# Split keys stacked from GpSimd's queue, split queries from SyncE's: four layers of attention on one core

## The chip, the cores and the metric

The program runs on one core of a Trainium2 chip. The metric is the device time of one execution in microseconds (us). One core has TensorE (PE) for matrix products, VectorE (DVE), ScalarE (ACT), GpSimd (POOL) and SyncE (SP). SP does no arithmetic here: its queue only issues transfers (DMAs). The DMA engines are shared by whoever issues.

## The reference

Sixteen batches of a 256 x 128 input pass through four layers. Layers 0, 2 and 3 hold attention with 16 heads of 8 channels; layer 1 is a mixture of experts with single-head attention. Cut to what matters here (heads are written out as an axis `h`):

```
q = (norm(x) @ Wq + bq)            # 256 queries, heads of 8
k = (norm(src) @ Wk + bk)          # 256 keys (self) or 1601 keys (cross, from the context)
v = (norm(src) @ Wv + bv)
attn = softmax(q @ k.T * 8**-0.5)  # per head, exact maximum subtracted
x = x + gate * (attn @ v @ Wo + bo)
```

Layer 0 is self attention, then cross attention with an MLP; layer 2 is cross attention; layer 3 is self attention, then cross attention with an MLP.

## The kernel before, in words

The program has four parts in a row: a small one that works out modulation columns, an attention phase `pa` (layer 0), the expert layer `moe` (layer 1) and an attention phase `pb` (layers 2 and 3). Only the two attention phases contain the change. Each runs two streams at once: `c`, the cross attention (1601 keys), and `z`, the self attention (256 keys). In `pa` both streams have 16 items (an item is one batch of one layer). In `pb` stream `c` has 32 (layer 2's batches, then layer 3's) and `z` has 16.

The work of a phase is cut into tokens: `S` and `T` are scores with their exponential, `V` the product with the values, `M` and `Rn` the maxima of the scores, `ln` a layer norm, `xt` a transpose of its result by PE, `q`, `k`, `v` the projections, `ca` the norm of the context, `ctx` its transposes, `proj` the output projection, `ln2`, `x2t`, `h`, `fc2` the MLP. `body_plan` writes down at which fraction of a steady body each token stands and of which item. A body is one round, in which the scores of one item of each stream are made while the next items are prepared. `stage_list` and `merge_maxima` turn that into one list, `PROG`. Every engine walks the same `PROG` in order, does the part of each token that is its own, and waits on semaphores for the others.

A query or key in f32 is split into three bf16 parts. ACT writes the projection to `kf`; POOL splits it into `ksp` (lines 914 to 920, token `k`), and likewise `qf` into `qsp` (lines 902 to 906, token `q`). The parts are then stacked on partitions by DMAs, so that one bf16 product gives the sum of six partial products: token `kq` (lines 597 to 610) issues 12 DMAs into `qst` and 12 into `kst`. Each moves 64 rows. A key row has 1601 numbers in stream `c` and 256 in `z`; a query row has 256. The stacks are double buffered, so `kq` of item i waits until PE has read the last score of item i - 2 (`last_score`).

Per body the order in `PROG` around the change is this. At the boundary of two bodies stand the last scores, `T` of `c`, and at once `kq` of `c` and `kq` of `z`. Then follow, among scores, values and maxima that concern only PE, ACT and DVE:

- in `pb`: `ln` of `c`, `ln` of `z`, `xt` of `c` (PE waits for `xn`, which POOL writes at line 887), `proj` of `c`, `q` of `c`, `xt` of `z`, `ca`, `proj` of `z`
- in `pa`: `ln` of `z`, `proj` of `c`, `ln2` of `c` (DVE waits for `x1`, which POOL writes at line 934), `xt` of `z`, `ca`, `proj` of `z`, `x2t` of `c`
- some 100 tokens after `kq`: the first `M` of the new item, where PE waits for both stacks (lines 1027 and 1028).

Each phase begins with bodies in which not all of this is present. `pa` has three bodies with a `z` item alone, then 13 with both streams at `kq`, then 3 with `c` alone. `pb` has 16 `kq` points with both streams and 16 with `c` alone.

Of the kernel before, what the change touches and what calls it, by code (L numbers as in the profile page):

```python
# [31 lines left out]
ROWS = 64  # L32
MAX_ROW = 62
K_PART = (0, 0, 0, 1, 1, 2)
# [14 lines left out]
def wait(eng, sem, value):  # L49

    if isinstance(value, int) and value < 1:
        return
    eng.wait_ge(sem, value)
# [121 lines left out]
K_ROWS = 48  # L175
# [250 lines left out]
def attention_phase(nc, nm, streams, cols_d, rows_d, ident_d, late_x, fill_late):  # L426
# [31 lines left out]
    def a_done(tok, s, i):  # L458

        return na[tok, s.key, i] + 1  # L460

    def last_score(s, i):
        return a_done(("T", QUADS - 1) if s.last < P else ("S", QUADS - 1, s.kt // 2 - 1, 1), s, i)

    with Semaphores(nc) as sems, ExitStack() as ctx:
# [3 lines left out]
        def sem(name):  # L469
            return sems(f"{nm}_{name}")  # L470
# [10 lines left out]
        for j, spec in enumerate(specs):  # L481
            w = spec.w = Weights()
# [60 lines left out]
        a_full, a_free = sem("act_ring_full"), sem("act_ring_free")  # L543
# [7 lines left out]
        @block.sync  # L551
        def _(sp):
            def const(dst, src, slow=False):
                sp.dma_start(dst, src, allow_slow_non_contiguous=slow).then_inc(consts, 16)

            def col(v):
                return v.rearrange("(c p) -> p c", p=P)

            def rows(v):
                return v.rearrange("(o n) -> o n", o=1).to_broadcast([P, D])  # L560

            const(ident[:], ident_d)
            for spec in specs:
                w = spec.w
                for dst, src in ((w.wq, spec.wq), (w.wk, spec.wk), (w.wv[:], spec.wv), (w.wo[:], spec.wo)):
                    const(dst, src)
                const(w.brow[:, 0, :], spec.bq.rearrange("(o n) -> o n", o=1))
                const(w.brow[:, 1, :], spec.bk.rearrange("(o n) -> o n", o=1))
                const(w.bv[:], col(spec.bv), slow=True)
                const(w.bo_rows[:], rows(spec.bo))  # L570
                if spec.mlp:
                    const(w.w1[:], spec.mlp["w1"])
                    const(w.w2[:], spec.mlp["w2"].rearrange("(c p) n -> p c n", p=P))
                    const(w.b1[:], col(spec.mlp["b1"]), slow=True)
                    const(w.b2_rows[:], rows(spec.mlp["b2"]))

            for tok, s, i in PROG:
                k, (spec, n), w = tok[0], s.items[i], i % 2
                if k == "ldx":
                    if spec.after:  # L580
                        key, first = spec.after
                        sp.wait_ge(by_key[key].x_out, 16 * (first + n + 1))
                    wait(sp, s.x_ln, i * QT)
                    sp.dma_start(s.xin[:], spec.x_src[n].rearrange("(t p) d -> p t d", p=P)).then_inc(s.x_in, 16)
                elif k == "lda":
                    if i:
                        sp.wait_ge(a_free, a_done(("xt",), s, i - 1))
                        if s.has_ctx:
                            sp.wait_ge(a_free, a_done(("ctx", len(s.groups) - 1), s, i - 1))
                    sp.dma_start(s.acols[:], cols_d[n]).then_inc(s.a_cols, 16)  # L590
                elif k == "ldc":
                    if i:
                        sp.wait_ge(a_full, a_done(("ctx", len(s.groups) - 1), s, i - 1))
                    src, kt = spec.ctx[n], s.kt
                    sp.dma_start(s.cin[:, 0:kt - 1, :], src[0:(kt - 1) * P, :].rearrange("(t p) d -> p t d", p=P)).then_inc(s.c_in, 16)
                    sp.dma_start(s.cin[0:s.last, kt - 1, :], src[(kt - 1) * P:s.keys, :]).then_inc(s.c_in, 16)
                elif k == "kq":
                    sp.wait_ge(s.filled, s.fills)
                    if i >= 2:
                        sp.wait_ge(a_full, last_score(s, i - 2))  # L600
                    sp.wait_ge(s.q_sp, i + 1)
                    for t in range(6):
                        for par in range(2):
                            lo = par * ROWS
                            sp.dma_start(s.qst[w][lo + t:lo + K_ROWS:6, :, :], s.qsp[lo:lo + ROWS, Q_PART[t], :]).then_inc(s.q_st, 16)
                    sp.wait_ge(s.k_sp, i + 1)
                    for t in range(6):
                        for par in range(2):
                            lo = par * ROWS
                            sp.dma_start(s.kst[w][lo + t:lo + K_ROWS:6, :, :], s.ksp[lo:lo + ROWS, K_PART[t], :]).then_inc(s.k_st, 16)  # L610
                elif k == "mr":
                    half = tok[1]
                    sp.wait_ge(a_free, a_done(("Rt", half), s, i))
                    for par in range(2):
                        at = par * ROWS + MAX_ROW
                        sp.dma_start(s.qst[w][at:at + 2, 4 * half:4 * half + 4, :], s.mrow[half][par * 8:par * 8 + 8, :]).then_inc(s.m_st[half], 16)
                elif k == "ldr":
                    wait(sp, s.d_x1, i)
                    wait(sp, s.d_x2, s.mlp_to[i])
                    sp.dma_start(s.xres[:], spec.x_src[n].rearrange("(t p) d -> p t d", p=P)).then_inc(s.x_res, 16)  # L620
                    if spec.gate is not None:
                        sp.dma_start(s.gate[:], rows_d[n][spec.gate:spec.gate + 1, :].to_broadcast([P, D])).then_inc(s.x_res, 16)
                    if spec.mlp:
                        sp.dma_start(s.dcols[:], cols_d[n]).then_inc(s.x_res, 16)
                        sp.dma_start(s.dgate[:], rows_d[n][spec.mlp["gate"]:spec.mlp["gate"] + 1, :].to_broadcast([P, D])).then_inc(s.x_res, 16)
                elif k == "st":
                    dst = spec.x_dst[n].rearrange("(t p) d -> p t d", p=P)
                    if spec.mlp:
                        sp.wait_ge(s.d_x2, s.mlp_to[i] + 1)
                        sp.dma_start(dst, s.x2[:]).then_inc(s.x_out, 16)  # L630
                    else:
                        sp.wait_ge(s.d_x1, i + 1)
                        sp.dma_start(dst, s.x1[:]).then_inc(s.x_out, 16)
            for s in streams:
                sp.wait_ge(s.x_out, 16 * len(s.items))

        @block.vector
        def _(dve):
# [41 lines left out]
            for tok, s, i in PROG:  # L680
                k, (spec, n) = tok[0], s.items[i]
                if k == "M":
                    _, p, u = tok
                    segs = s.units[u]
                    cnt, width = len(segs), segs[0][2]
# [177 lines left out]
        def _(pool):  # L863
# [10 lines left out]
            for tok, s, i in PROG:  # L874
                k, (spec, n) = tok[0], s.items[i]
                w = spec.w
# [30 lines left out]
                elif k == "k":  # L907
# [12 lines left out]
                    ins = pool.tensor_tensor(s.ksp[:, 2, part], s.kf[:, part], s.ksp[:, 1, part], ALU.subtract)  # L920
                    if tok[1] == len(s.groups) - 1:
                        ins.then_inc(s.k_sp, 1)
                elif k == "proj":
                    pool.wait_ge(a_free, a_done(tok, s, i))
                    pool.wait_ge(s.x_res, s.res_to[i + 1] * 16)
# [45 lines left out]
        def _(pe):  # L971
# [9 lines left out]
            for tok, s, i in PROG:  # L981
                k, (spec, n), b2 = tok[0], s.items[i], i % 2
                w = spec.w
                if k in ACT_RING:
                    N = na[tok, s.key, i]
                    dst = aunit[N % RING_A]
                    wait(pe, a_free, N - RING_A + 1)
                if k == "S":
                    _, q, j, pp = tok
                    pair = 2 * q + pp  # L990
                    if j == 0 and pp == 0 and q % 2 == 0:
# [8 lines left out]
                elif k == "T":  # L1000
# [6 lines left out]
                    ins.then_inc(a_full, 1)  # L1007
                elif k == "V":
                    _, q, t = tok
                    tail = s.last < P and t == s.kt - 1  # L1010
                    if t == 0:
# [813 lines left out]
```

## Time and profile before

| | |
|---|---|
| median of 3 runs | 5429.4 us (5426.66 to 5432.44) |
| the profiled execution | 5426.89 us, span of the trace 5425.1 us |
| PE busy | 4676.3 us (86% of the span) |
| DVE busy | 4123.3 us (76%) |
| ACT busy | 3587.5 us (66%) |
| POOL busy | 1673.2 us (31%) |
| mean granted TensorE clock | 0.965 of full speed |

The profile counts an engine's compute instructions as busy, not its waits and not the issuing of DMAs. The span is the time from the first to the last instruction; the execution's own time is 1.8 us longer.

### The profile page before, as it was taken

The page shows a single profiled execution, that of the slowest core. Times are in us where ns is not written, and L with a number is a line of the kernel's source. Part 1 is how long each engine was busy: PE and PEld are TensorE (multiplying, and loading weights), DVE is VectorE, ACT ScalarE, POOL GpSimd, SP SyncE. Part 2 cuts the span into 40 slices and gives each one's busy share as a digit, 9 for nine tenths or more (in the row PEclk, how much of TensorE's full clock was granted, in tenths as well). Part 3 has the DMA queues.
Part 4 walks back from the last instruction along what each step waited for, and adds up shares of the span by engine and source line. Part 5 has one row for each costly group of instructions (what it writes and reads, how often), then busy time and mean ns, then how long its engine had stood idle before and what let it go on. Part 6 is the DMA issues. An engine that isn't in the chain of part 4 may idle for free.

```text
span 5425.1 us, 123295 instructions
## 1 busy us (share of the span) xinstructions
PE 4676.3 (86%) x47956; PEld 2196.8 (40%) x47956; DVE 4123.3 (76%) x8997; ACT 3587.5 (66%) x4899; POOL 1673.2 (31%) x2339
## 2 busy tenths in 40 slices
PE   4689889889998588867989999999999998989987
PEld 2234433433433377752333333333333343333333
DVE  4588888888878244445888888888888887887884
ACT  1377777777777344423777777777777777777776
POOL 3444343343341100024232423233222223232321
PEclk9799999999999899986999999999999999999998
DMA  2211211211210111102112111121211111211110
GB/s 52 68 52 54 68 44 54 67 44 52 61 39 25 45 33 33 33 25 64 52 51 66 55 58 55 53 66 54 67 56 53 51 48 50 62 43 53 42 46 7
DMA packets 362976, 271.12 MB, mean 50 GB/s; under 512 B 47911, under 2 KB 325002, under 8 KB 362396
## 3 DMA queue, kind: packets, MB, share of 16 engines
q1 hardware_dynamic: 362396, 263.23, 17.0%
q8 instruction: 383, 6.28, 0.5%
q14 instruction: 197, 1.61, 0.1%
HBM read 86.96 MB, written 12.78 MB: 18 GB/s over the span
## 4 chain that ended last, share of the span: by engine, by line
PE 36%; ACT 7%; DVE 6%; issue 5%; POOL 1%; SPq 0%; DMA 0%; ACTq 0%; POOLq 0%; DVEq 0%
PE pb_obank L1021 13%; PE pb_dbank L1034 8%; ACT pb_probs L772 6%; DVE pb_c_maxs L693 5%; PE pb_aunit L997 5%; PE pb_aunit L1068 2%; PE pb_aunit L1075 2%; PE pb_dbank L1082 1%; PE pb_aunit L1060 1%; PE pb_aunit L1108 1%; PE pb_aunit L1102 1%; PE pb_aunit L1005 1%; ACT pb_c_kf L815 1%; PE pb_aunit L1051 0%; PE pb_aunit L1092 0%
## 5 line engine op out<-in xcount | busy, mean ns | idle before, releaser
L693 DVE TENSOR_REDUCE pb_c_maxs<-pb_dbank 128x1 f32<-128x512 f32 (+1 forms) x3584 | 2044.5, 627 | 411.6 <-PE pb_dbank L1034 397.1
L772 ACT ACTIVATE pb_probs<-pb_aunit 128x1024 f32<-128x1024 f32 (+1 forms) x1792 | 1744.5, 1024 | 380.4 <-PE pb_aunit L997 344.8
L693 DVE TENSOR_REDUCE pa_c_maxs<-pa_dbank 128x1 f32<-128x512 f32 (+1 forms) x1792 | 1025.8, 627 | 180.2 <-PE pa_dbank L1034 170.5
L772 ACT ACTIVATE pa_probs<-pa_aunit 128x1024 f32<-128x1024 f32 (+1 forms) x960 | 934.8, 1026 | 198.1 <-PE pa_aunit L997 174.8
L1021 PE MATMUL pb_obank<-pb_probs,pb_c_vaug 128*9 128x256 f32 x13312 | 953.2, 384 | 6.3 <-ACT pb_probs L772 5.5
L1034 PE MATMUL pb_dbank<-pb_c_kst,pb_c_qst 62*128 62x512 bf16 (+1 forms) x4096 | 780.5, 344 | 77.1 <-DVE pb_c_maxs L693 67.7
L997 PE MATMUL pb_aunit<-pb_c_qst,pb_c_kst 64*128 64x256 bf16 x6144 | 570.1, 273 | 61.1 <-ACT pb_probs L772 43.1
L1034 PEld LDWEIGHTS pb_dbank<-pb_c_kst,pb_c_qst 62*128 62x128 bf16 x4096 | 233.6, 93 | 632.8 <-DVE pb_c_maxs L693 433.2
L1021 PE MATMUL pa_obank<-pa_probs,pa_c_vaug 128*9 128x256 f32 x6656 | 481.2, 385 | 6.2 <-ACT pa_probs L772 5.8
L1034 PE MATMUL pa_dbank<-pa_c_kst,pa_c_qst 62*128 62x512 bf16 (+1 forms) x2048 | 396.8, 345 | 53.8 <-DVE pa_c_maxs L693 42.6
L1021 PEld LDWEIGHTS pb_obank<-pb_probs,pb_c_vaug 128*9 128x9 f32 x13312 | 245.1, 89 | 375.3 <-issue 214.4
L997 PEld LDWEIGHTS pb_aunit<-pb_c_qst,pb_c_kst 64*128 64x128 bf16 x6144 | 253.2, 95 | 309.8 <-ACT pb_probs L772 134.1
L879 POOL TENSOR_SCALAR pb_c_rs_v<-pb_c_agg 128x2 f32<-128x2 f32 x32 | 7.9, 246 | 1032.9 <-DVE pb_c_agg L714 1032.9
L997 PE MATMUL pa_aunit<-pa_c_qst,pa_c_kst 64*128 64x256 bf16 x3072 | 285.5, 272 | 36.4 <-ACT pa_probs L772 25.9
L1034 PEld LDWEIGHTS pa_dbank<-pa_c_kst,pa_c_qst 62*128 62x128 bf16 x2048 | 115.4, 93 | 331.1 <-DVE pa_c_maxs L693 213.2
L693 DVE TENSOR_REDUCE pa_z_maxs<-pa_dbank 128x2 f32<-128x512 f32 x256 | 163.9, 686 | 107.7 <-PE pa_dbank L1034 107.7
L1021 PEld LDWEIGHTS pa_obank<-pa_probs,pa_c_vaug 128*9 128x9 f32 x6656 | 121.4, 89 | 191.0 <-issue 111.4
L997 PEld LDWEIGHTS pa_aunit<-pa_c_qst,pa_c_kst 64*128 64x128 bf16 x3072 | 122.6, 95 | 168.8 <-ACT pa_probs L772 91.6
L693 DVE TENSOR_REDUCE pb_z_maxs<-pb_dbank 128x2 f32<-128x512 f32 x256 | 164.6, 685 | 23.6 <-PE pb_dbank L1034 23.4
L914 POOL CAST pb_c_ksp<-pb_c_kf 128x1024 bf16<-128x1024 f32 x64 | 54.6, 852 | 288.6 <-ACT pb_c_kf L815 288.6
L1526 DVE SCALAR_TENSOR_TENSOR moe_hh<-moe_ht,moe_hz 128x512 f32<-128x512 f32 x48 | 33.2, 692 | 123.6 <-ACT moe_ht L1620 123.6
L926 POOL TENSOR_TENSOR pb_c_x1a<-pb_c_x1a,pb_l_cross_bo_rows 128x256 f32<-128x256 f32 x32 | 23.2, 724 | 337.0 <-ACT pb_c_x1a L842 337.0
(475 smaller groups left out, 6680.3 us busy)
## 6 DMA issues: line engine op xcount, KB each, us to landing
pb_c_kst<-pb_c_ksp SPq DMA_DIRECT2D x384, 200.1 KB
pa_c_kst<-pa_c_ksp SPq DMA_DIRECT2D x192, 200.1 KB
pb_c_cin<-in_ctx SPq DMA_DIRECT2D x32, 768.0 KB
pa_c_cin<-in_ctx SPq DMA_DIRECT2D x16, 768.0 KB
moe_cin<-in_ctx SPq DMA_DIRECT2D x16, 768.0 KB
pb_c_qst<-pb_c_qsp SPq DMA_DIRECT2D x384, 32.0 KB
pa_z_qst<-pa_z_qsp SPq DMA_DIRECT2D x192, 32.0 KB
pa_z_kst<-pa_z_ksp SPq DMA_DIRECT2D x192, 32.0 KB
```

The costliest lines, as they stand in the source:

```text
L693: dve.tensor_reduce(dst, dbank[N % RING_D][:, 0:cnt * width].rearrange("p (s c) -> p s c", s=cnt), AX.X, ALU.max).then_inc(d_free, 1)
L772: act.activation(probs[u % RING_P][0:rows].rearrange("p a i q -> p (a i q)"), src[0:rows, :], ACT.Exp, scale=HD ** -0.5).then_inc(a_free, 1)
L815: act.activation(s.kf[:, at:at + width], src[:, 0:width], ACT.Identity, bias=w.bk[:]).then_inc(a_free, 1)
L914: pool.tensor_copy(s.ksp[:, 0, part], s.kf[:, part]).then_inc(s.k_hi, 1)
L997: ins = pe.matmul(dst[:, par * 512 + h * NQ:par * 512 + (h + 1) * NQ], s.kst[b2][lo:lo + ROWS, pair, t * P:(t + 1) * P], s.qst[b2][lo:lo + ...
L1005: ins = pe.matmul(dst[0:s.last, par * 512 + pp * NQ:par * 512 + (pp + 1) * NQ], s.kst[b2][lo:lo + ROWS, 2 * q + pp, (s.kt - 1) * P:s.keys] ...
L1021: ins = pe.matmul(obank[32 * h4:32 * h4 + HD + 1, half * NQ:(half + 1) * NQ], s.vaug[i % 2][:, t, 4 * q + h4, :], src, start=(t == 0), sto ...
L1034: ins = pe.matmul(dbank[nd[tok, s.key, i, par] % RING_D][:, col:col + width], s.qst[b2][lo:lo + MAX_ROW, p, qt * P:(qt + 1) * P], s.kst[b2 ...
L1060: ins = pe.transpose(dst[:, (t - t0) * P:(t - t0) * P + rows], s.cin[0:rows, t, :], ident[0:rows, 0:rows])
L1068: ins = pe.matmul(dst[:, at - t0 * P:at - t0 * P + width], w.wkp[:], src[:, at:at + width], start=True, stop=True)
L1075: ins = pe.matmul(dst[0:rows, (t - t0) * P:(t - t0 + 1) * P], (s.srct if s.has_ctx else s.xmt)[:, t * P:t * P + rows], w.wv[:], start=True ...
L1082: ins = pe.transpose(dbank[N % RING_D][:, g * P:(g + 1) * P], s.osb[:, g, qt * P:(qt + 1) * P], ident[:])
```

## The change

`kq` now appears on two engines. SP keeps the 12 DMAs of the queries, with their waits. POOL's branch of `PROG` gets a `kq` of its own: it waits for the fills of the stacks, for the last score of item i - 2 and for its own last split of the keys, and then issues the same 12 key DMAs from POOL's queue. Nothing that computes is changed.

```diff
                         for par in range(2):
                             lo = par * ROWS
                             sp.dma_start(s.qst[w][lo + t:lo + K_ROWS:6, :, :], s.qsp[lo:lo + ROWS, Q_PART[t], :]).then_inc(s.q_st, 16)
-                    sp.wait_ge(s.k_sp, i + 1)
-                    for t in range(6):
-                        for par in range(2):
-                            lo = par * ROWS
-                            sp.dma_start(s.kst[w][lo + t:lo + K_ROWS:6, :, :], s.ksp[lo:lo + ROWS, K_PART[t], :]).then_inc(s.k_st, 16)
                 elif k == "mr":
...
                         ins.then_inc(s.k_sp, 1)
+                elif k == "kq":
+                    w = i % 2
+                    pool.wait_ge(s.filled, s.fills)
+                    if i >= 2:
+                        pool.wait_ge(a_full, last_score(s, i - 2))
+                    pool.wait_ge(s.k_sp, i + 1)
+                    for t in range(6):
+                        for par in range(2):
+                            lo = par * ROWS
+                            pool.dma_start(s.kst[w][lo + t:lo + K_ROWS:6, :, :], s.ksp[lo:lo + ROWS, K_PART[t], :]).then_inc(s.k_st, 16)
                 elif k == "proj":
```

## Rows read from the trace of the kernel before

**Rows 1.** Windows, one body of pb with both streams
```profile
core 0: us, PE busy (x) PEld busy (x) DVE busy (x) ACT busy (x) POOL busy (x), PEclk, DMA share, GB/s
3518.70:3613.70 95.00, 86.48 (x977) 36.45 (x969) 82.59 (x187) 71.80 (x91) 31.92 (x49) 1.00 0.20 58
```

**Rows 2.** Instructions of line 610: issue times in ns, and who waited
```profile
L610 SPq DMA_DIRECT2D pb_c_kst<-pb_c_ksp x384: 611/1018/1871, 2467.3 to 5258.8; - x192
L610 SPq DMA_DIRECT2D pb_z_kst<-pb_z_ksp x192: 612/612/761, 2798.5 to 4223.6; - x192
...
  ACT pa_z_kf L815: 20.6, 3
  PE pa_dbank L1034: 9.4, 1
  PE pb_dbank L1034: 3.6, 1
```

**Rows 3.** Waits of SP's queue: us in total, times, longest
```profile
SPq L616 <- ACT pb_c_mrow L833: 1311.0, 64, 39.9
```

**Rows 4.** Timeline of SP around kq, the same body of pb
```profile
3517.30 1.26 SPq L616 DMA_DIRECT2D pb_c_qst<-pb_c_mrow  x2
3518.68 7.96 SPq L605 DMA_DIRECT2D pb_c_qst<-pb_c_qsp  x12
3526.69 12.88 SPq L610 DMA_DIRECT2D pb_c_kst<-pb_c_ksp  x12
3539.68 8.38 SPq L605 DMA_DIRECT2D pb_z_qst<-pb_z_qsp  x12
3548.10 8.15 SPq L610 DMA_DIRECT2D pb_z_kst<-pb_z_ksp  x12
3569.05 1.36 SPq L616 DMA_DIRECT2D pb_c_qst<-pb_c_mrow  x2
```

**Rows 5.** Timeline of POOL, the same body
```profile
3530.67 0.25 POOL L879 TENSOR_SCALAR pb_c_rs_v<-pb_c_agg 128x2 f32<-128x2 f32 x1 [38.92 <-DVE pb_c_agg L714]
...
3532.16 0.88 POOL L887 TENSOR_SCALAR pb_c_xn<-pb_c_xin,pb_c_rs_m,pb_c_rs_y 128x128 f32<-128x128 f32 x2
...
3554.94 2.46 POOL L894 TENSOR_TENSOR pb_c_cs_y<-pb_c_cs_v,pb_mhalf 128x13 f32<-128x13 f32 x1
```

**Rows 6.** Timeline of PE, same body: last score, xt of c, first M of new item
```profile
3518.20 0.41 PE L1005 MATMUL pb_aunit<-pb_c_qst,pb_c_kst 64*65 64x256 bf16 x4
...
3539.10 0.44 PE L1047 MATMUL pb_aunit<-pb_ident,pb_c_xn 128*128 128x128 f32 x2 [0.30 <-ACT pb_c_vaug L827]
...
3566.60 0.39 PE L1034 MATMUL pb_dbank<-pb_c_kst,pb_c_qst 62*128 62x512 bf16 x2
```

**Rows 7.** Timelines of SP, POOL, DVE and PE, one body of pa
```profile
841.59 7.90 SPq L605 DMA_DIRECT2D pa_c_qst<-pa_c_qsp  x12
...
944.09 7.90 SPq L605 DMA_DIRECT2D pa_c_qst<-pa_c_qsp  x12
...
956.19 0.24 POOL L879 TENSOR_SCALAR pa_z_rs_v<-pa_z_agg 128x2 f32<-128x2 f32 x1 [25.23 <-DVE pa_z_agg L714]
...
957.67 0.88 POOL L887 TENSOR_SCALAR pa_z_xn<-pa_z_xin,pa_z_rs_m,pa_z_rs_y 128x128 f32<-128x128 f32 x2
967.01 0.73 POOL L926 TENSOR_TENSOR pa_c_x1a<-pa_c_x1a,pa_l_cross_bo_rows 128x256 f32<-128x256 f32 x1 [8.46 <-ACT pa_c_x1a L842]
967.81 0.74 POOL L934 TENSOR_TENSOR pa_c_x<-pa_c_x1a,pa_c_xres 128x256 f32<-128x256 f32 x1
...
973.00 0.47 DVE L744 BATCH_NORM_STATS2 pa_c_st<-pa_c_x 128x6 f32<-128x128 f32 x2
...
973.17 0.44 PE L1047 MATMUL pa_aunit<-pa_ident,pa_z_xn 128*128 128x128 f32 x2 [0.68 <-ACT pa_probs L772]
```

**Rows 8.** Timelines of SP and PE, one body of pb with c alone
```profile
4722.99 7.93 SPq L605 DMA_DIRECT2D pb_c_qst<-pb_c_qsp  x12
...
4740.87 0.44 PE L1047 MATMUL pb_aunit<-pb_ident,pb_c_xn 128*128 128x128 f32 x2 [0.46 <-ACT pb_c_vaug L827]
...
4808.44 7.90 SPq L605 DMA_DIRECT2D pb_c_qst<-pb_c_qsp  x12
```

**Rows 9.** Timeline of all engines, start of pb
```profile
2467.27 12.72 SPq L610 DMA_DIRECT2D pb_c_kst<-pb_c_ksp  x12
2467.33 0.25 POOL L879 TENSOR_SCALAR pb_c_rs_v<-pb_c_agg 128x2 f32<-128x2 f32 x1
...
2469.87 0.66 PE L1047 MATMUL pb_aunit<-pb_ident,pb_c_xn 128*128 128x128 f32 x2 [9.89 <-POOL pb_c_xn L887]
...
2486.22 0.61 PE L1034 MATMUL pb_dbank<-pb_c_kst,pb_c_qst 62*128 62x512 bf16 x2 [3.57 <-DMA pb_c_kst<-pb_c_ksp]
```

**Rows 10.** Timeline of all engines, start of pa
```profile
62.88 0.67 POOL L920 TENSOR_TENSOR pa_z_ksp<-pa_z_kf,pa_z_ksp 128x256 bf16<-128x256 f32 x1
...
69.43 10.77 POOL L867 MEMSET pa_c_kst<- 128x12808 bf16 x1
...
83.68 0.67 POOL L920 TENSOR_TENSOR pa_z_ksp<-pa_z_kf,pa_z_ksp 128x256 bf16<-128x256 f32 x1
...
90.81 0.69 PE L1047 MATMUL pa_aunit<-pa_ident,pa_z_xn 128*128 128x128 f32 x2 [0.69 <-ACT pa_probs L772]
```

**Rows 11.** Waits of all engines, first 350 us
```profile
ACT pa_z_qf L794 <- DMA pa_z_qst<-pa_z_qsp: 23.9, 3, 17.5
```

## The prediction

> **What bounds the kernel now.** I read the window of one whole body first, then who waits for the stacks, then SP's waits, and last the timelines of SP, POOL and PE around the point where the key transfers are issued.
>
> In a steady body of pb PE is busy 86.5 us of 95.0, DVE 82.6, ACT 71.8 and POOL 31.9, at full granted clock [rows 1]. So PE sets the pace, in the order of its list. The key transfers don't touch it: PE waited for a key stack exactly twice in the whole run, 9.4 and 3.6 us, both at the start of a phase; ACT waited for it three times, 20.6 us together, at the start of pa [rows 2]. SP isn't short of time either: it spent 1311 us waiting at its next job, the rows of maxima [rows 3]. In the body shown its 48 issues end at 3556.3 and its next issue is at 3569.05 [rows 4]. Taking 24 of the 48 away from SP therefore gives nothing in a steady body.
>
> **What the change puts on POOL.** A POOL that is busy 31.9 us of 95 looks free, but what counts is where its idle time lies. It finished its last split at 3491.7 (3530.67 less the 38.92 it was idle) and next works at 3530.67, on c's layer norm [rows 5]. Its new DMAs can't use the first 27 us of that gap. They wait for the last score of the item that used the buffer before, which PE finishes at 3518.20 + 0.41 = 3518.6 [rows 6]; SP began at 3518.68 for the same reason [rows 4]. Both streams have their `kq` there, so 24 issues run back to back on POOL from 3518.6, and the norms of c and z stand behind them in its queue.
>
> **The price of one issue.** No row shows a DMA issued by POOL. The bounds come from the nearest rows:
> - from below, SP's issue of the same 64 rows where nothing holds it back: 0.61 us [rows 2];
> - from above, the longest POOL instruction on few elements: 2.46 us [rows 5].
>
> I take 1.02 us, the median of SP's issue of the c keys [rows 2]. It lies nearer to the lower end because the job is the same, 64 rows on each side. I take it for z too, since a queue that is served by software should pay by the row and not by the byte. So 12 issues are 12.2 us and 24 are 24.5 us.
>
> The Trainium skill bears on this in "DMA: Bandwidth & Descriptors", Specifications and SWDGE vs HWDGE: DMAs from GpSimd get their descriptors from code on GpSimd's own cores, those from SP from dedicated hardware, with first bytes after about 1 us against about 0.6. The 0.61 us of SP's row agrees with the second figure; the first would make 24 issues 24 us, an estimate from that page and close to mine. That GpSimd's cores do the issuing is what puts the norms behind it; no run here shows that yet.
>
> **pb, both streams (16 points).** c's norm takes from 3530.67 to 3532.16 + 0.88 = 3533.04, 2.4 us, and PE takes its result at 3539.10 [rows 5, 6]. Room for issues: 3539.1 - 3518.6 - 2.4 = 18.1 us. Needed 24.5, so PE stands 6.4 us in each such body. I count it in full. PE is the engine that sets the pace, DVE and ACT can't run ahead of it by more than their few banks, and the next batch of issues hangs on PE's own last score, so the delay moves on with it. 16 x 6.4 = 102 us.
>
> **pa, both streams (13 points).** c's norm stands elsewhere in that list. First after the issues come z's norm (2.4 us) and then c's x1 (1.5 us, two instructions). DVE wants x1 at 973.0 and PE z's norm at 973.17, with issues from 944.1 on [rows 7]. The tighter room is 973.0 - 944.1 - 2.4 - 1.5 = 25.0 us, needed 24.5: nothing lost, and only 0.5 us to spare.
>
> **c alone (16 points in pb, 3 in pa).** Room: 4740.9 - 4723.0 - 2.4 = 15.5 us [rows 8]; needed 12.2. Nothing lost.
>
> **Start of pb.** The split ends, 12 issues take 12.2 us, and only then comes the norm that began at 2467.33 and for which PE waited 9.89 us. PE's first maxima stood 3.57 us for the key stack anyway [rows 9]. So 12.2 - 3.6 = 9 us.
>
> **Start of pa.** The first z items pass one after the other through split, issue, norm, transpose and split, with little else to do. POOL has its split ready at 63.6, then 12 issues, a norm and the fills of c's stacks, whose last one ran from 69.43 to 80.2 and will now end some 12 us later. The split that ended at 84.35 ends at 96.6, 12 more issues bring 108.8, the norm 111.2, and PE transposes at about 111 in place of 90.81: 20 us late [rows 10]. Some of that comes back. ACT had waited 20.6 us for z's key stacks [rows 2] and 23.9 for z's query stacks, which stood in SP's queue behind the c keys [rows 11]. Two more batches of issues follow. I take 20 us net, with 0 and 49 (four batches of 12.2, nothing given back) as the ends.
>
> **Sum.** 102 + 0 + 0 + 9 + 20 = 131 us on the profiled execution's 5426.9 us, 5558. The median of the runs is 2.5 us above that execution, so I say 5560 us.
>
> The landing of the keys isn't a term. In a c body they are all issued by 3518.6 + 24.5 = 3543, earlier than SP's last at 3556.3 [rows 4], and even SP's were never waited for in a steady body [rows 2].
>
> **The rivals.**
> - *Not slower.* If one issue on POOL costs 0.75 us or less, or if issuing doesn't occupy the cores that compute, 24 issues fit in the 18.1 us of pb and no body is stretched. What is left is the start of pa, where keys and queries are now issued side by side and ACT's waits of 44.5 us shrink, against POOL's later norms. Time: 5415 to 5435. For it speaks SP's 0.61 us; against it that POOL would have to issue nearly as fast. The skill's rule for this ("DMA: Bandwidth & Descriptors", Issuing engines are not separate DMA queues) is that issuing from several engines saves only sequencer time, usually small. Taken alone it says no change, since the row of SP's waits shows that its time is free.
> - *A dearer issue, and pa is bound too.* From 1.04 us on pa's 13 bodies pay as well, from 1.29 us (15.5 / 12) those with c alone. At 1.4 us: 16 x (33.6 - 18.1) = 248, 13 x (33.6 - 25.0) = 112, 16 x (16.8 - 15.5) = 21, starts 45: 426 us, 5855. At the upper bound of 2.46 us the same lines give 654 + 442 + 224 + 80, some 6830 us. For it speaks that POOL's short instructions cost more than their data explain, 0.25 us for two columns and 2.46 for thirteen [rows 5]; against it that nothing else about 64 rows is slow.
> - *The keys land late.* If a transfer issued by POOL took so long that the last were in after the first maxima of the new item, PE would wait at line 1028. They have from 3543 to the first maxima at 3566.6, over 23 us [rows 6], where SP needs 12.9 us for all twelve of c [rows 4]. I give it little.
>
> **How the numbers follow.** Forecast, an issue between 0.75 and 1.25 us: 0.62, by itself 5445 to 5730 (at 1.25: 190 + 65 + 45 = 300 us). Dearer issue: 0.24. Not slower: 0.11. Late keys or something else: 0.03. The range runs from 5450 to 5860: it leaves out the not-slower case and most of what lies beyond 1.4 us. A difference of 0.2% (11 us) is about what a measurement of this kernel can tell from none. The not-slower case splits into 0.03 faster and 0.06 same, its remainder being a small loss at the starts; so slower has 0.91.
>
> **What would show it.** In the trace of the changed kernel: POOL's queue with DMA issues of about 1 us, 12 or 24 in a row, beginning at PE's last score; c's norm in pb starting some 24 us after it; PE waiting some 6 us at line 1047 for `pb_c_xn` in 16 bodies, each about 101 us long; bodies of pa at 102.5 us as before (841.59 to 944.09) and those with c alone at 85.4 [rows 7, 8]. Wrong would be an issue time far from 1.02 us (each 0.1 us is worth 38 us, above 1.04 us 70), a stall that PE makes up for later in the body, or bodies of pa stretched at an issue time below 1.04 us.

## The result and the profile after

The changed kernel takes 5450.9 us (median of 5 runs, 5449.3 to 5452.5) against 5430.6 us (5426.7 to 5432.9) for the kernel before, run beside it: a ratio of 1.0036 with a 95% interval from 1.0024 to 1.0048. It is slower, as I forecast, but by 20 us and not by 131. 5450.9 lies at the lower edge of my range, and that is chance: as shown below, what slows the kernel stands in none of my terms.

First the price of one issue. In the view of the new line 927 on POOL, the three numbers are shortest, median and longest issue in ns; below them stand idle times of POOL ahead of these instructions, in us and times.

```profile
L927 POOL DMA_DIRECT2D pb_c_kst<-pb_c_ksp x384: 562/562/667, 2472.2 to 5270.3; - x192
L927 POOL DMA_DIRECT2D pa_z_kst<-pa_z_ksp x192: 561/561/769, 63.6 to 1367.1; - x192
...
  issue: 502.9, 36
  PE pb_aunit L1010: 446.3, 17
```

One issue takes 0.56 us, for 200 KB of c and for 32 KB of z alike. That is below SP's fastest, 0.61 [rows 2], which I had taken for the lower bound. Twelve take 6.8 us and twenty-four 13.4.

The windows view of the body that answers to [rows 1], then POOL's and PE's timelines around it [rows 5, 6] and SP's [rows 4]:

```profile
3535.10:3630.10 95.00, 86.48 (x977) 36.53 (x977) 82.62 (x186) 71.79 (x91) 45.30 (x73) 1.00 0.26 58
```
```profile
3535.64 6.77 POOL L927 DMA_DIRECT2D pb_c_kst<-pb_c_ksp  x12 [27.46 <-PE pb_aunit L1010]
3542.40 6.64 POOL L927 DMA_DIRECT2D pb_z_kst<-pb_z_ksp  x12
3549.12 0.25 POOL L874 TENSOR_SCALAR pb_c_rs_v<-pb_c_agg 128x2 f32<-128x2 f32 x1
```
```profile
3534.66 0.41 PE L1010 MATMUL pb_aunit<-pb_c_qst,pb_c_kst 64*65 64x256 bf16 x4
3555.55 0.44 PE L1052 MATMUL pb_aunit<-pb_ident,pb_c_xn 128*128 128x128 f32 x2 [0.30 <-ACT pb_c_vaug L822]
```
```profile
3535.14 14.16 SPq L605 DMA_DIRECT2D pb_c_qst<-pb_c_qsp  x12
3549.41 7.82 SPq L605 DMA_DIRECT2D pb_z_qst<-pb_z_qsp  x12
```

POOL is busy 13.4 us more, which are its 24 issues (on POOL the profile counts them as busy), and PE, DVE and ACT are busy as before, within 0.03 us, in the same 95.0 us. The order of events is the forecast one: 24 issues from the last score on, then c's norm. But the norm starts 14 us after the score, not 24, and PE takes its result 20.9 us after that score began, as in [rows 6]. SP now needs 14.2 us for c's queries in place of 8.0, with key transfers beside them; in pb nobody waits for a query stack.

So where do 25.6 us of span (5450.7 against 5425.1) come from? The two profiled executions lie 5 us further apart than the medians. I took from SP's timeline of both traces when the query issues of each item of c begin, and subtracted:

```
item of c, stage            before     after      later by
7th body of pa              739.00     737.24     -1.8
12th body of pa             1251.36    1249.31    -2.1
first of pb                 2455.06    2459.06     4.0
third of pb                 2608.81    2617.03     8.2
third body with z           2949.02    2958.20     9.2
the next                    3043.96    3060.44    16.5
eight bodies on             3803.88    3820.32    16.4
the next                    3898.05    3920.29    22.2
last                        5238.58    5263.62    25.0
```

The loss is made at a few places: between the stages, in the start of pb, and in two single bodies of pb with both streams. The other bodies of that kind cost nothing. The body that begins at 2958.2 shows what those two have in common. POOL's timeline, then PE's, then windows of PE with its granted clock (the number behind the busy time):

```profile
2958.71 6.77 POOL L927 DMA_DIRECT2D pb_c_kst<-pb_c_ksp  x12 [27.45 <-PE pb_aunit L1010]
2965.47 2.77 POOL L927 DMA_DIRECT2D pb_z_kst<-pb_z_ksp  x5
2976.84 3.88 POOL L927 DMA_DIRECT2D pb_z_kst<-pb_z_ksp  x7 [8.60 <-issue]
2980.79 0.25 POOL L874 TENSOR_SCALAR pb_c_rs_v<-pb_c_agg 128x2 f32<-128x2 f32 x1
```
```profile
2983.31 0.66 PE L1052 MATMUL pb_aunit<-pb_ident,pb_c_xn 128*128 128x128 f32 x2 [5.35 <-POOL pb_c_xn L882]
```
```profile
2980.00:2982.00 2.00, 0.00 (x0) 1.00 0.24 66
2982.00:2984.00 2.00, 0.69 (x6) 0.50 0.00 0
...
2988.00:2990.00 2.00, 2.00 (x22) 0.79 0.00 0
2990.00:2992.00 2.00, 2.00 (x23) 1.00 0.00 0
```

After its 17th issue in this body POOL pauses for 8.6 us, for no reason that the profile names. With the pause the issues last 22.0 us; that is more than the room of 18.1, and PE waits 5.35 us for the norm. Behind that idle stretch its granted clock is 0.50, which is 1.2 GHz, until about 2989; in the kernel before it is 1.00 from 2561 to 4480, through all bodies of this kind. Wait and clock together make the body 102.2 us long instead of 94.9. The other long body, at 3820.3, has its pause (7.86 us) behind the 17th issue too.

Counting POOL's key transfers through the trace, a pause stands behind the 113th of a phase and then behind every 108th: 8 in all. Four, behind five issues of a body, took 2.0 us each, as this one:

```profile
3440.70 2.89 POOL L927 DMA_DIRECT2D pb_c_kst<-pb_c_ksp  x5 [27.44 <-PE pb_aunit L1010]
3445.62 3.88 POOL L927 DMA_DIRECT2D pb_c_kst<-pb_c_ksp  x7 [2.03 <-issue]
```

The other four took 7.9 to 9.3 us. Only two of those fell into a pb body with both streams, where there is no room for them. The one in pa (9.3 us at 859) is covered by the 25.0 us there, and that of 8.1 us at 5101, in a body with c alone, takes 14.8 us with its 12 issues, out of a room of 15.5: PE didn't wait for the norm.

The start of pb answers to [rows 9], on POOL and PE:

```profile
2472.16 6.77 POOL L927 DMA_DIRECT2D pb_c_kst<-pb_c_ksp  x12 [0.62 <-POOL pb_c_ksp L915]
2479.00 0.25 POOL L874 TENSOR_SCALAR pb_c_rs_v<-pb_c_agg 128x2 f32<-128x2 f32 x1
```
```profile
2481.53 0.66 PE L1052 MATMUL pb_aunit<-pb_ident,pb_c_xn 128*128 128x128 f32 x2 [17.25 <-POOL pb_c_xn L882]
```

The norm stands behind 6.8 us of issues; PE waits 17.25 us in place of 9.89, and no longer for the keys. Net of the 3.57 us that it waited for them before, that is 3.8. By SP's query issues, the second item of pb begins 4.3 us later against the kernel before than the first did.

Last, the boundary from pa to the next stage, in the timelines of the kernel before and of the changed one: the last store of pa, and POOL's first instruction behind it.

```profile
1819.55 0.37 SPq L630 DMA_DIRECT2D x_after<-pa_c_x  x1
1822.78 0.10 POOL L1633 MEMSET moe_mhalf<- 128x2 f32 x1 [3.25 <-POOLq L85]
```
```profile
1820.62 0.37 SPq L625 DMA_DIRECT2D x_after<-pa_c_x  x1
1826.83 0.10 POOL L1638 MEMSET moe_mhalf<- 128x2 f32 x1 [6.24 <-POOLq L85]
```

Line 85 is the barrier at the end of a stage, behind the handing back of its semaphores. POOL stands there 3.0 us longer.

### The profile page after: what moved, and what is told of

Read it like the earlier page. It is cut to its first block, busy times and chain, and to the rows that moved or that the text cites. A ratio compares the mean times of both kernels' runs of the same rounds, so it can differ in the third digit from the quotient of the medians.

```text
span 5450.7 us, 123375 instructions
## 1 busy us (share of the span) xinstructions
PE 4689.4 (86%) x47956; PEld 2201.9 (40%) x47956; DVE 4129.8 (76%) x8997; ACT 3588.2 (66%) x4899; POOL 2209.1 (41%) x3299
## 4 chain that ended last, share of the span: by engine, by line
PE 36%; ACT 7%; DVE 6%; issue 5%; POOL 2%; ACTq 0%; DMA 0%; SPq 0%; POOLq 0%; DVEq 0%
PE pb_obank L1026 13%; PE pb_dbank L1039 8%; ACT pb_probs L767 5%; DVE pb_c_maxs L688 5%; PE pb_aunit L1002 5%; PE pb_aunit L1073 2%; PE pb_aunit L1080 2%; PE pb_aunit L1065 1%; PE pb_dbank L1087 1%; PE pb_aunit L1113 1%; PE pb_aunit L1107 1%; PE pb_aunit L1010 1%; ACT pb_c_kf L810 1%; PE pb_aunit L1056 0%; PE pb_aunit L1097 0%
## 5 line engine op out<-in xcount | busy, mean ns | idle before, releaser
L927 POOL DMA_DIRECT2D pb_c_kst<-pb_c_ksp x384 | 216.5, 571 | 730.0 <-PE pb_aunit L1010 446.3
L688 DVE TENSOR_REDUCE pb_z_maxs<-pb_dbank 128x2 f32<-128x512 f32 x256 | 164.6, 685 | 24.5 <-PE pb_dbank L1039 24.3
L927 POOL DMA_DIRECT2D pa_c_kst<-pa_c_ksp x192 | 108.3, 571 | 184.3 <-issue 184.3
```

Source lines behind the costliest of these rows:

```text
L688: dve.tensor_reduce(dst, dbank[N % RING_D][:, 0:cnt * width].rearrange("p (s c) -> p s c", s=cnt), AX.X, ALU.max).then_inc(d_free, 1)
L927: pool.dma_start(s.kst[w][lo + t:lo + K_ROWS:6, :, :], s.ksp[lo:lo + ROWS, K_PART[t], :]).then_inc(s.k_st, 16)
```

## The experiments

The theory from the two traces: issuing takes 0.56 us and fits in the room, so most bodies are free; what is lost is lost where something else stands in POOL's list beside the issues (a norm in the start of pb, a pause in two bodies), and at the boundary. Nine kernels test it and its rivals; the first four were written from these two traces, the others from what came before them.

**z's issues behind the norms.** In pb, POOL's list keeps `kq` of c where it is and gets that of z behind the next norm of z:

```
-            for tok, s, i in PROG:
+            for tok, s, i in pool_order(PROG, nm):     # pb: ("kq") of z put behind the next ("ln") of z
```

> In pb, POOL's list has the issues of z's keys behind the layer norms of c and z; c's keys stay ahead of them. Nothing else is moved. Theory (issuing fits in the room, and what is lost in the two long bodies at 2958 and 3820 us is POOL's pause of some 8 us, which pushes c's norm past the point where PE wants it): only 12 issues (6.8 us) and at most one pause (9 us) stand ahead of the norm, 16 of the 18.1 us of room, so both bodies are back at 95 us and the time is 5436 to 5441 us. Rival (the loss is made by transfers that run beside each other, or by PE's clock, not by POOL's order): the same number of transfers and issues, so 5448 to 5453 us, and long bodies as before.

Measured: 5438.9 us (11 runs, 5434.1 to 5442.2), ratio 1.0011 (1.0003 to 1.0020). POOL and PE in the body that was long:

```profile
2958.25 6.79 POOL L943 DMA_DIRECT2D pb_c_kst<-pb_c_ksp  x12 [27.41 <-PE pb_aunit L1026]
2969.38 0.25 POOL L890 TENSOR_SCALAR pb_c_rs_v<-pb_c_agg 128x2 f32<-128x2 f32 x1 [4.34 <-DVE pb_c_agg L725]
...
2974.14 2.87 POOL L943 DMA_DIRECT2D pb_z_kst<-pb_z_ksp  x5
2978.69 3.89 POOL L943 DMA_DIRECT2D pb_z_kst<-pb_z_ksp  x7 [1.69 <-issue]
```
```profile
2977.80 0.44 PE L1068 MATMUL pb_aunit<-pb_ident,pb_c_xn 128*128 128x128 f32 x2 [0.30 <-ACT pb_c_vaug L838]
```

Both long bodies are back at 94.9 and 94.2 us, and the same transfers are made. So it was POOL's order. The time came as expected. The pause itself is shorter too: 1.7 us behind 5 issues of z, where c's twelve ended 9 us earlier.

**pb alone.** In pa SP issues the keys again.

```
+                    if nm == "pa":
+                        ... the key transfers on sp, as before the change
-                elif k == "kq":
+                elif k == "kq" and not (nm == "pa"):
```

> In pa SP issues the keys as before the change, in pb POOL does. Theory: the change loses 3.0 us at the boundary from pa to the next stage (a gap of 6.2 us in place of 3.3, where POOL's queue is closed) and wins about as much at the start of pa, where keys and queries go out side by side; so the time stays at 5448 to 5453 us, the gap at the boundary is 3.3 us again and pa begins its steady part some 3 us later. Rival (the start of pa costs, as I forecast, and is hidden in the sum by something else): 5431 to 5440 us.

Measured: 5452.0 us (5 runs, 5446.2 to 5454.2), ratio 1.0034 (1.0022 to 1.0047). The gap at the boundary is 3.27 us again, and by SP's query issues the seventh body of pa begins 2.9 us later than in the changed kernel. Both are as expected, and so is the median: what pa wins at its start and what it loses at its end are each of some 3 us, and their sum can't be told from nothing.

**All on POOL, and half the rows.** The first has the queries issued by POOL as well, 48 issues in a body with both streams. The second also has 48, but by cutting each key transfer in two:

```
-    pool.dma_start(s.kst[w][lo + t:lo + K_ROWS:6, :, :], s.ksp[lo:lo + ROWS, K_PART[t], :])
+    for h in range(2):
+        at = lo + t + 24 * h
+        pool.dma_start(s.kst[w][at:at + 19:6, :, :], s.ksp[lo + 32 * h:lo + 32 * h + 32, K_PART[t], :])
```

> POOL issues the queries too: 24 issues for one item, 48 in a body with both streams. Theory (an issue takes 0.56 us and holds POOL's list up, and c's norm behind it has room for 18.1 us in pb and 25.0 in pa): 48 issues take 26.9 us, so 16 bodies of pb pay 8.8 us each (141) and 13 of pa 1.9 each (25); c alone, 13.4 against 15.5 us, nothing; and now the pauses, one every 108 transfers, fall into bodies that have no room left and count in full: 12 or 13 of them at 2 to 9 us, 25 to 110 us. Together 5640 to 5730 us, bodies of pb about 104 us. Rival (issuing lies beside POOL's other work, and the norm isn't held up): 5445 to 5460 us.

> Each key transfer on POOL is cut into two of 32 rows: 24 issues for an item, the same bytes and rows. If an issue is paid by its rows (as I assumed), it takes 0.28 to 0.35 us, the time stays at 5445 to 5470 us, and the pauses come every 216 issues. If it is paid by the instruction, it stays near 0.56 us: 48 take 26.9 us, bodies of pb are stretched by 8.8 us, and the time is 5610 to 5730 us. Whether the pauses come after 108 or 216 issues tells a limit on instructions from one on rows.

Measured: 5695.0 us (4 runs, 5693.3 to 5701.9), ratio 1.0485 (1.0471 to 1.0499), and 5767.6 us (5 runs, 5757.1 to 5777.9), ratio 1.0622 (1.0607 to 1.0636). All on POOL, a body of pb without a pause:

```profile
3584.57 6.76 POOL L920 DMA_DIRECT2D pb_c_qst<-pb_c_qsp  x12 [27.40 <-issue]
...
3604.62 6.64 POOL L925 DMA_DIRECT2D pb_z_kst<-pb_z_ksp  x12
3611.34 0.25 POOL L867 TENSOR_SCALAR pb_c_rs_v<-pb_c_agg 128x2 f32<-128x2 f32 x1
```
```profile
3613.87 0.66 PE L1050 MATMUL pb_aunit<-pb_ident,pb_c_xn 128*128 128x128 f32 x2 [10.04 <-POOL pb_c_xn L875]
```

Half the rows, the issue line:

```profile
L929 POOL DMA_DIRECT2D pb_c_kst<-pb_c_ksp x768: 588/591/688, 2556.0 to 5580.2; - x192
```

With 48 issues there is an edge near the one that I had worked out: 26.7 us of issues, PE waits 9.5 to 12.3 us for the norm in each of the 16 pb bodies, and most of them take 106 to 107 us. Those with c alone stay at 85.5. The total lies in the expected range, but its parts are others than expected. The pauses took 0.3 to 2.0 us and cost little, the stalls were larger than 8.8 us, and the last store of pa already came 61 us later than in the kernel before. In pa three bodies in a row still took 102.6 us, so the room there is more than 25.0 us. An issue of 32 rows takes 0.59 us, no less than one of 64: POOL is paid by the instruction, not by the row. The time, 5767.6 us, is 38 us above the range that I had given for that reading. This kernel comes nearest to the one that I had forecast, with 28 us of issues in a body where I had said 24.5. PE's wait at c's norm is 11.84 us in one of its pb bodies, most of them last 107 to 109 us, and those of pa 102 to 110.

**A point close to the edge.** The queries of c on POOL too, those of z with SP: 36 issues.

```
+                    if s.has_ctx:
+                        pool.wait_ge(s.q_sp, i + 1)
+                        ... the twelve query transfers of c on pool, ahead of its keys
```

> POOL issues the queries of c too, those of z stay with SP: 36 issues in a body with both streams, 24 in one with c alone. Theory (a room of 18.1 us ahead of c's norm in pb, 25.0 in pa, 15.5 with c alone): 36 issues take 20.3 us, which is 2.2 too much in pb and fits in pa; 24 take 13.5 and fit. 16 bodies of pb pay 2.2 us, with PE's lower clock behind each wait perhaps 3, so 35 to 48 us; the start of pb pays 6.8 more for the twelve queries ahead of its norm. 5490 to 5515 us, bodies of pb 97 to 98.5 us, those of pa 102.4 and of c alone 85.4 as before. Rival (there is no such edge; what 48 issues cost comes from POOL being busy at all): half of the way from 24 to 48 issues, about 5573 us, and bodies of pa longer too.

Measured: 5539.0 us (4 runs, 5536.1 to 5539.6), ratio 1.0201 (1.0187 to 1.0215), a miss by 24 us above the 5490 to 5515 expected, and 34 below the rival's 5573. The steady bodies of pa stay at 102.5 and those of c alone at 85.5, against the rival: only pb is over an edge. But most pb bodies take 98 to 101 us, not 97 to 98.5. By the third item of pb the run is 25 us behind the kernel before, and the bodies with both streams add nearly all of the rest. PE's wait in the body at 3588.7, and windows of it behind the wait:

```profile
3611.41 0.41 PE L1060 MATMUL pb_aunit<-pb_ident,pb_c_xn 128*128 128x128 f32 x2 [3.09 <-POOL pb_c_xn L884]
```
```profile
3610.00:3612.00 2.00, 0.59 (x10) 1.00 0.62 118
3612.00:3614.00 2.00, 2.00 (x18) 0.50 0.00 0
3614.00:3616.00 2.00, 2.00 (x18) 0.65 0.00 0
3616.00:3618.00 2.00, 2.00 (x25) 1.00 0.00 0
```

The issues lasted 20.1 us, 2.0 over the room; PE waited 3.1, which is 2.8 more than the 0.3 that it waits at this place before the change [rows 6], and then ran for about 3.4 us at half its clock, which loses 1.7. Together 4.5, and the body is 4.5 longer. With 48 issues it is the same sum: 8.6 over, 9.7 more waited, the body 11.5 longer. So the room is 17.0 us and not 18.1, and each stall costs nearly 2 us on top through the clock. The traces say where the 1.1 us are. POOL's first issue begins 0.57 us after the score and not at once, 0.23 us lie around the norm (between the last issue and it, and between it and PE), and PE was ready 0.30 us before the 3539.10 that I had read.

**What the change costs, taken away.** pa by SP; in pb z's issues behind the norms, and those of c's first item behind c's second norm:

```
+        if tok[0] == "kq" and (not s.has_ctx or i == 0) and ...:      # held back in POOL's order
```

> Built from what the runs say costs something: in pa SP issues the keys (no dearer boundary to the next stage), in pb POOL does, with the keys of z behind the norms of c and z in every body and those of c's first item behind c's second norm. Theory (all that the change costs is the boundary, the first norm of pb and the two bodies in which a pause pushes c's norm): nothing of it is left, 5428 to 5438 us, not to be told from the kernel before, and PE waits for the first norm of pb about 10 us in place of 17. Rival (moving the keys costs something everywhere, as by transfers that get in each other's way): 5440 to 5450 us.

Measured: 5433.0 us (11 runs, 5425.9 to 5439.1), ratio 1.0006 (0.9998 to 1.0015), as expected and not to be told from the kernel before. PE waits for the first norm as before:

```profile
2473.63 0.66 PE L1074 MATMUL pb_aunit<-pb_ident,pb_c_xn 128*128 128x128 f32 x2 [9.91 <-POOL pb_c_xn L904]
```

From the second item of pb to the last, the query issues begin 0.6 to 1.4 us later than in the kernel before. POOL makes 576 key transfers in pb, with its five pauses (two of them cut to 1.7 us by the new order), and the time is that of the kernel before. Nothing is won, and nothing was to be won: SP's time was never short [rows 3].

**The boundary.** One single key transfer of pa begun by POOL in the kernel before:

```
+                    if nm == "pa" and s.has_ctx and i == 0:
+                        pool.dma_start(s.kst[0][ROWS + 5:ROWS + K_ROWS:6, :, :], s.ksp[ROWS:2 * ROWS, K_PART[5], :])
```

> The kernel before with one single transfer of a key stack (the last of c's first item in pa) begun by POOL, all the others by SP. Theory (closing a stage in which POOL's queue has begun transfers costs 3 us, however many there were): the gap behind the last store of pa is 6.2 us in place of 3.3, the time 5432 to 5437 us. Rival (the 3 us grow with the number of transfers, as a queue that has to be cleaned up): the gap is 3.3 to 3.4 us and the time that of before. The other steps stay as in the kernel before.

Measured: 5428.0 us (11 runs, 5419.9 to 5434.4), ratio 0.9995 (0.9986 to 1.0004). The gap is 3.26 us, so my theory of a fixed price for a used queue fell. The two halves of the change, next, give two more points.

**One stream at a time.**

```
-                elif k == "kq":
+                elif k == "kq" and not s.has_ctx:     # or: and s.has_ctx; the other stream's keys stay with sp
```

> POOL issues the keys of z alone, SP those of c as before: 192 transfers of 32 KB in each of the two stages. Theory: 12 issues take 6.8 us and fit everywhere, also with a pause of 9 us ahead of c's norm (16 of 18.1), so 5426 to 5436 us, no difference. What a pause waits for: if it lasts until the transfers that POOL has outstanding are in, no pause is longer than about 2 us here, since little data is under way; if its length goes by count (short and long in turn, 2 and 8 to 9 us, as in the changed kernel), every second one is long here too. The boundary behind pa, if its length goes by the number of POOL's transfers in the stage (1: 3.3 us, 384: 6.2, 576 and 768: 9.2), has 3.3 or 6.2 us.

> The other half: POOL issues c's keys alone, SP those of z: 192 transfers of 200 KB in pa, 384 in pb. Theory: 6.8 us, with a pause at most 16, fit in the 18.1 us; both long bodies of the changed kernel are gone; what stays is the first norm of pb behind 12 issues, 4 us, and 0 or 3 us at the boundary: 5433 to 5441 us. Rival (it is the transport of the large c stacks beside SP's queries that costs, not POOL's list): 5445 to 5453 us, since nearly all of the bytes are still in this half. The pauses, if they wait for data under way, come to 8 us or more where some c transfers are outstanding and the engines are busy.

Measured: z's keys alone 5440.9 us (11 runs, 5434.2 to 5448.3), ratio 1.0022 (1.0013 to 1.0031); c's alone 5435.3 us (11 runs, 5431.2 to 5440.0), ratio 1.0012 (1.0003 to 1.0021). The second came as expected, against the rival: the half with nearly all the bytes costs less. The first is a miss by 5 us. All its steady bodies of pb are 94 to 95 us; it begins its first c item 6 us late (171.8 against 165.4 us), and its boundary takes 7.8 us, where I had expected 3.3 or 6.2. The boundary of c's half takes 7.8 us too. The first pause in pb with z's keys alone, that with c's keys alone, and the boundary with z's:

```profile
3630.20 2.89 POOL L933 DMA_DIRECT2D pb_z_kst<-pb_z_ksp  x5 [29.78 <-issue]
3636.78 3.88 POOL L933 DMA_DIRECT2D pb_z_kst<-pb_z_ksp  x7 [3.69 <-issue]
```
```profile
3236.45 2.89 POOL L933 DMA_DIRECT2D pb_c_kst<-pb_c_ksp  x5 [27.44 <-PE pb_aunit L1016]
3247.20 3.88 POOL L933 DMA_DIRECT2D pb_c_kst<-pb_c_ksp  x7 [7.86 <-issue]
```
```profile
1832.84 0.10 POOL L1644 MEMSET moe_mhalf<- 128x2 f32 x1 [7.79 <-POOLq L85]
```

With transfers of 32 KB the two pauses were 3.0 and 3.7 us, with those of 200 KB all four were 6.4 to 11.0. That speaks for a pause that waits until data under way is in. The landing times in the traces bear it out for the long ones: in the changed kernel, with z's issues behind the norms, with half the rows and in these two halves, all 15 pauses of 3.0 us and more within a batch of issues ended 0.05 to 1.64 us after the last transfer that POOL had begun was in. It isn't the whole rule: the four pauses of 2.0 us in the changed kernel ended with three of their five transfers still under way. What makes a pause of one kind or the other is open.

## Why the prediction was wrong in size

**The bound.** Right. SP gains nothing, and the steady bodies hang on PE's list. In the kernel with the costs taken away the whole of pb has the pace of the kernel before.

**The price of one issue.** This is the step that failed: "I take 1.02 us", and with it the lower bound of 0.61. It measured 0.56, so 24 issues needed 13.4 us and not 24.5, and they fit in the room instead of exceeding it by 6.4. I had bounded a new operation from below by another engine's row, as if POOL could not be quicker. The argument that a queue served by software "should pay by the row" is refuted as well: 32 rows cost 0.59 us and 64 cost 0.56. The Trainium skill had the right reading in "Perfetto Trace Analysis", DMA Instruction — SWDGE (GPSIMD): the profile's end of such an instruction is the end of writing descriptors, not of the data's movement. The trace agrees, 0.56 us of issue for 6.7 us to landing and no difference between 32 and 200 KB. I had instead set first-byte figures of that skill beside my price and SP's 0.61 us, and a latency is not the time for which an engine is held.

**pb, both streams.** The mechanism was right: norms behind the issues, PE stalled by what goes over the room. The room was 1.1 us too wide. The term was 16 x 6.4 = 102 us. Its stall happened in none of the 14 bodies without a pause behind the 17th issue; the 13.1 us measured come from the two with one. Where the issues do exceed the room (36 and 48 of them), the stall is there in every body, and larger than by my sum, by 1.1 to 1.4 us of wait and nearly 2 us of clock. "I count it in full" was too low: at my own 24.5 us a body would have been some 9 us longer and not 6.4, an estimate from the rows with 36 and 48 issues. Two errors stood in the term, and the smaller one pulled against the larger.

**pa and c alone.** Nothing was lost, as forecast: bodies of 102.4 and 85.4 us. With 13.4 us of issues the margin in pa was 11.6 us, not 0.5.

**Start of pb.** 9 us forecast, 4.3 measured: the same sum with 6.8 us in place of 12.2 gives 3.2. The way was right, the size hung on the price.

**Start of pa.** 20 us forecast; the seventh body begins 1.8 us earlier than before. The delay came as I traced it: with 6.8 us for each of the two batches the second norm should end 10 us later than before and not 20, near 101, and POOL's row has it:

```profile
100.09 0.88 POOL L882 TENSOR_SCALAR pa_z_xn<-pa_z_xin,pa_z_rs_m,pa_z_rs_y 128x128 f32<-128x128 f32 x2
```

c's first item still begins 6.1 us late, but its second 3.7 us early. More comes back than was lost. Keys and queries are issued side by side, and ACT waits 3.9 us for z's query stacks in place of 23.9 [rows 11] and no longer for its key stacks, 20.6 us before [rows 2]. That the z half alone begins 6 us late and the c half on time fits: z pays, c gives back. "20 us net" had set what comes back against two more batches of delay, as if they were equal.

**Not foreseen.** The pauses (13 us in two bodies) and the boundary (3 us) appear in none of my terms. With the true price my sum would have had a few us at the starts and nothing else. The rival *Not slower*, whose condition (0.75 us or less) was met, gave 5415 to 5435 and missed the measured time for the same reason. Steps of 1 to 3 us remain between the two traces. One of them is not the change's: the body at 5089.67 takes 88.5 us with stretches of 6.8 and 3.4 us at a granted clock of 0.50, and the kernel before has such a body as well, 88.1 us at 4893.88, with the same two stretches; its neighbours have one of 3.4 us and take 85.4. The others are not traced to a cause.

## What to carry to other kernels

Work moved to another engine's queue costs what it pushes back there: find the next instruction behind it that the pacing engine needs, and subtract. Here it was free up to the edge, and beyond it each body paid the overshoot plus some 3 us. So what stands behind the issues in that queue matters as much as their number: the same 24 issues were free with half of them behind the norms, pauses and all. Where an operation has no row in the trace, another engine's row is no lower bound; forecast the case below it as well, and work out from what price on the edge is met.

## What the runs showed of the hardware

- A DMA issued by POOL holds it for 0.56 us with 64 rows, whether they carry 32 or 200 KB together, and for 0.59 us with 32 rows. SP's issue of the same transfer took 0.61 to 1.87 us.
- POOL's issuing pauses at a regular count of transfers. In the changed kernel the first pause is behind the 113th of a phase, then one every 108th; with c's keys alone every 113th. With queries and keys of both streams most of the pauses seen are 84 or a multiple of it apart, with half the rows mostly 96. So the limit is not on rows, which would have given 216, and not on the number of instructions alone. Pauses took from under 0.5 to 11.0 us. Those of 3.0 us and more ended within 1.64 us after all of POOL's transfers were in; some shorter ones did not wait for that.
- The end of a stage took 3.3 us with none or one transfer begun by POOL in pa, 7.8 with 192 (of z or of c alike), 6.2 with 384, and 9.2 with 576 or 768. The 192 of z carry a sixth of the bytes of c's 192 and cost the same. It doesn't rise steadily with the number; the rule is open.
- After PE had waited 3 to 18 us for a norm in a body of pb with both streams, it worked on at a granted clock of 0.50 for 3 to 6 us. In waits of 9 us and more the clock fell during the wait, in those of 3 to 4 us between 0.5 us before its end and 1.6 us behind it.
